# A two-layer graph attention and a transformer block on one core: a loop over batches written out from a table, wide products between the first batch's steps, setup work in other places

## The reference

```python
x = x + gat2(ctx_512, layernorm(x))      # adjacency = the normalised x
x = x + block(layernorm(x))

def gat_layer(x, adj, W, a_self, a_neigh, b):        # 8 heads of 32
    feat = einsum('nf,hfo->hno', x, W)
    e = (feat @ a_self)[:, :, None] + (feat @ a_neigh)[:, None, :]
    e = leaky_relu(e, 0.2) + -1e10 * (1.0 - adj)[None]
    out = softmax(e, -1) @ feat + b[:, None, :]
    return elu(out.transpose(1, 0, 2).reshape(256, 256))

# block: rmsnorm; q (16 heads of 128), k, v (4 heads); rmsnorm and rotary of q and k;
# causal attention; output projection; rmsnorm; gate of 8 experts, top 2;
# eight silu-gated experts of 176, mixed by the gate; residuals
```

## Time and profile before

| | |
|---|---|
| median of 3 runs | 676.4 us (676.07 to 676.8) |
| the profiled execution: time, span | 676.07 us, 676.1 us |
| instructions | 11574 |
| busy: TensorE, its weight loads | 604.8 us (89%), 445.9 us (66%) |
| busy: VectorE, ScalarE, GpSimd | 441.0 (65%), 266.7 (39%), 292.0 us (43%) |
| mean granted TensorE clock | 0.944 |
| moved by DMA | 14.51 MB, nearly all in the first 35 us |

### The profile page before, as it was taken

How to read it: one execution, slowest core, us unless ns; L and a number is a source line. 1 busy time by engine, 2 the same in 40 slices (tenths; PEclk the granted TensorE clock), 3 DMA queues, 4 the chain that set the end, 5 groups by cost and what they waited for, 6 DMA issues and landing times.

```text
span 676.1 us, 11574 instructions
## 1 busy us (share of the span) xinstructions
PE 604.8 (89%) x3140; PEld 445.9 (66%) x3140; DVE 441.0 (65%) x1277; ACT 266.7 (39%) x653; POOL 292.0 (43%) x588
## 2 busy tenths in 40 slices
PE   2786938979999998879999998879999998999998
PEld 1573933559678873558778973458777974676786
DVE  5727537975738756985738765986738766565363
ACT  2313305546533304636633304647633303674020
POOL 1514325885424023886425023886424126773000
PEclk9997558898999998979999998989999999999999
DMA  8900000000000000000000000000000000000000
GB/s 313 380 6 0 2 16 4 1 2 1 0 1 2 2 26 10 4 0 2 0 1 1 1 26 10 1 0 1 1 1 1 1 1 16 1 1 1 1 1 16
DMA packets 8305, 14.51 MB, mean 21 GB/s; under 512 B 860, under 2 KB 7068, under 8 KB 7988
## 3 DMA queue, kind: packets, MB, share of 16 engines
q1 hardware_dynamic: 8244, 13.76, 5.8%
HBM read 12.70 MB, written 1.05 MB: 20 GB/s over the span
## 4 chain that ended last, share of the span: by engine, by line
PE 56%; DVE 16%; issue 13%; POOL 9%; ACT 4%; POOLq 1%; DMA 1%; DVEq 0%; ACTq 0%; SPq 0%
PE bank L565 10%; PE bank L463 9%; PE ob L443 9%; PE bank L523 5%; PE tb L432 5%; PE bank L542 4%; DVE tt L904 3%; POOL m L775 2%; PE bank L538 2%; PE bank L534 2%; PE bank L509 2%; DVE lr L895 2%; PE zb L424 1%; ACT prob L666 1%; PE zb L414 1%
## 5 line engine op out<-in xcount | busy, mean ns | idle before, releaser
L735 POOL TENSOR_SCALAR tt<-tt,gmn 128x256 f32<-128x256 f32 x128 | 77.1, 613 | 64.1 <-DVE gmn L904 63.5
L509 PE MATMUL bank<-wqkv_sb,hT 128*128 128x512 f32 x192 | 97.9, 648 | 0.0
L666 ACT ACTIVATE prob<-bank,sneg,rms 128x128 f32<-128x128 f32 (+1 forms) x128 | 64.0, 507 | 68.5 <-DVE sneg L995 67.7
L775 POOL TENSOR_TENSOR m<-early,rope_s 128x256 f32<-128x256 f32 x80 | 70.8, 908 | 42.1 <-ACT early L647 41.8
L463 PE MATMUL bank<-m,wgu_sb 128*128 128x128 f32 (+1 forms) x480 | 86.6, 330 | 1.0 <-DVE m L1025 0.6
L791 POOL TENSOR_SCALAR prob<-prob,srcp 128x128 f32<-128x128 f32 (+1 forms) x128 | 53.7, 436 | 55.5 <-DVE srcp L1066 55.4
L463 PEld LDWEIGHTS bank<-m,wgu_sb 128*128 128x128 f32 x480 | 71.2, 191 | 9.2 <-issue 2.2
L443 PEld LDWEIGHTS ob<-feat,gpT 128*128 128x128 f32 x512 | 75.8, 227 | 0.8 <-issue 0.6
L443 PE MATMUL ob<-feat,gpT 128*128 128x33 f32 x512 | 75.2, 297 | 0.0
L895 DVE SCALAR_TENSOR_TENSOR lr<-zs 128x512 f32<-128x512 f32 x64 | 50.9, 797 | 25.3 <-ACT zs L625 22.6
L904 DVE CUSTOM_DVE_ANT_0 tt<-lr,maskv 128x256 f32<-128x256 f32 x128 | 62.3, 522 | 3.5 <-issue 2.9
(11 more groups left out here) (151 smaller groups left out, 1026.5 us busy)
## 6 DMA issues: line engine op xcount, KB each, us to landing
wqkv_sb<-wqkv_dram SPq DMA_DIRECT2D x1, 3072.0 KB, 12.4
wgu_sb<-wgu_dram SPq DMA_DIRECT2D x2, 1408.0 KB, 11.2
wo_sb<-wo_dram SPq DMA_DIRECT2D x1, 2048.0 KB, 17.8
wd_sb<-wd_dram SPq DMA_DIRECT2D x1, 1408.0 KB, 15.6
xin<-x_dram SPq DMA_DIRECT2D x4, 256.0 KB, 2.7
out_dram<-rows SPq DMA_DIRECT2D x8, 128.0 KB, 1.9
rows<-gat_rows_dram SPq DMA_DIRECT2D x1, 512.0 KB
cst<-consts_dram SPq DMA_DIRECT2D x1, 425.0 KB, 3.6
```

Source lines behind the costliest of these rows:

```text
L509: mm = pe.matmul(ps[:, :], hT[:, k, t * P:(t + 1) * P], wqkv_sb[:, k, c * G * HD:(c + 1) * G * HD], start=(k == 0), stop=(k == KT - 1))
L666: ins = act.activation(prob[:, n % 5, i * nk:(i + 1) * nk], ps[:, i * nk:(i + 1) * nk], ACT.Exp, bias=sneg[:, n, i:i + 1], scale=rq(g, t, ...
L735: ins = pool.tensor_scalar(tt[:, k % 3, h, :], tt[:, k % 3, h, :], -1.0, gmn[:, k % 3, h:h + 1], ALU.mult, ALU.add)
L775: ins = pool.tensor_tensor(dst[:, :, c, :], src[:, :, 1 - c, :], s_, ALU.mult)
```

## The change

- The loop is gone: a table `PLAN` lists ("gat", b, step), ("prep", b, step) and ("tail", b, step), and each engine issues its work by walking it. All semaphore values are constants. The order is the loop's, but what follows the second layer, now `prep`, is issued two steps earlier for batch 0 (`PREP_LEAD`).
- `keep_clock(n)` issues n products of 128x512 in bf16 into a bank that is not in use yet, after a step's `gat` work, for batch 0 alone: 127 in all, by the table `WAKE`.
- `apply_terms(1)` moves from after step 2 to after steps 14 and 15, one half of the weights each; the rotary tables and casts from after step 24 to after steps 25, 26 and 27. VectorE waits for the small loads at step 12.
- For batch 0 the three Newton rounds of the normalisation behind the layers are done on VectorE.
- `x1` and its statistics exist twice, the moments of that normalisation, `go`, `gT` have tiles of their own, `hn` lies in `m2`, `mixT` in `partsT`; the constants that only tables need are loaded into `x1[1]` and `hid` and not kept.

```diff
+SEQ, XS = (0, 1, 2, 3), 2
+PREP_LEAD = 2
+TERMS1_AT, ROPE_AT = (14, 15), (25, 26, 27)
+WAKE = {1: 2, 2: 4, 5: 2, 6: 2, 7: 2, 8: 14, 18: 5, 20: 3, 22: 3, 24: 6, 28: 3, 29: 3, 30: 3, 31: 12, 41: 18, 43: 6, 45: 3}
+WAKE.update({s: 2 for s in tuple(range(9, 18)) + tuple(range(32, 41))})
...
+PLAN = []
+for step in range(STEPS):
+    PLAN += [("gat", 0, step), ("prep", 0, step + PREP_LEAD)]
+for batch in range(B):
+    for step in range(STEPS):
+        PLAN += [("gat", batch + 1, step), ("prep", batch + 1, step)] if batch + 1 < B else []
+        PLAN += [("tail", batch, step)]
...
+            def keep_clock(n):
+
+                for _ in range(n):
+                    pe.matmul(bank[BANKS - 1][:, :], identb[:, :], identb[:, :].unsqueeze(1).broadcast_to([P, 4, P]), start=True, stop=True)
+
...
-            with pe.Fori(0, B - 1) as b:
-                for s in range(STEPS):
-                    gat(b + 1, s)
+            for what, b, s in PLAN:
+                if what == "gat":
+                    if b == 0 and s == TERMS_AT[1]:
+                        pe.wait_ge(setup_done, 2)
+                    gat(b, s)
+                    if b == 0:
+                        keep_clock(WAKE.get(s, 0))
+                elif what == "prep":
+                    prep(b, s)
+                else:
...
-                dve.wait_ge(dve_a, b * N_A + count[0])
+                dve.wait_ge(dve_a, count[0])
...
+                    if b == 0:
+                        for _ in range(3):
+                            newton(link_a, b, ln_y[:, :], ln_a[:, :], ln_v[:, :])
+                        dve.sem_inc(ln_ready, 1)
                     dve.sem_inc(ln_seed, 1)
...
+            def setup(s):
+
+                if s == UNIT_AT[0][-1]:
+                    dve.wait_ge(in_gat, 128)
+                if s in TERMS1_AT:
+                    apply_terms(1, TERMS1_AT.index(s))
+                if s == TERMS1_AT[1]:
+                    dve.sem_inc(setup_done, 1)
+                if s in ROPE_AT[:2]:
+                    rope_tables(ROPE_AT.index(s))
+                if s == ROPE_AT[2]:
+                    link(dve.tensor_copy(causal[:, :], causal_in))
+                    link(dve.tensor_copy(expert_rows[:, :], spread_in))
+                    dve.sem_inc(setup_done, 1)
...
-            for s in range(STEPS):
-                gat(0, s)
-                if s == PARTS_AT[0]:
-                    dve.wait_ge(in_gat, 80)
-                    apply_terms(1)
-                    dve.sem_inc(setup_done, 1)
-                if s == PARTS_AT[1]:
-                    rope_tables()
```

More of the change, by code:

```diff
@@ L43 @@
 C_TRI = C_NEIGH + 1
-C_END = C_TRI + E * E
+C_KEPT = C_TRI + E * E
+C_COS = C_KEPT
+C_SIN = C_COS + T * HD
+C_CAUSAL = C_SIN + T * HD
+C_END = C_CAUSAL + P
 def constants():
@@ L255, in block_program @@
         mixp = sb("mixp", [P, T, NP, E], BF16)
-        mixT = sb("mixT", [NP * E, N], BF16)
+        mixT = partsT[0:NP * E, :]
         th = pT1[:, :, :, :].rearrange("p m h q -> p (m h q)")[:, 0:3 * N].rearrange("p (a n) -> p a n", a=3)
@@ L361, in _ @@
             sp.dma_start(wd_sb[:, :, :], wd.rearrange("(j p) n -> p j n", p=P)).then_inc(in_d, 16)
[L363 to L374, removed]
             load_inputs(1)
-            with sp.Fori(0, B - 2) as b:
-                load_inputs(b + 2)
+            for b in range(B):
+                if b + 2 < B:
+                    load_inputs(b + 2)
                 store(b)
-            store(B - 2)
-            store(B - 1)
             sp.wait_ge(out_free, 16 * T * (B + 1))
@@ L600, in _ @@
                     long_products(b, s)
-            for s in range(STEPS):
-                for w in work(s):
-                    fill(B - 1, w)
-                long_products(B - 1, s)
         @block.scalar
@@ L682, in empty @@
                     act.activation(th[:, n % 3, :], ps[:, 0:N], ACT.Tanh, scale=0.5).then_inc(tanh_ready, 1)
-            for s in range(STEPS):
-                gat(0, s)
-            act.wait_ge(setup_done, 3)
-            with act.Fori(0, B - 1) as b:
-                for s in range(STEPS):
-                    gat(b + 1, s)
+            for what, b, s in PLAN:
+                if what == "gat":
+                    gat(b, s)
+                elif what == "tail":
+                    if b == 0 and s == 0:
+                        act.wait_ge(setup_done, 3)
                     for w in use(s):
                         empty(b, w)
-            for s in range(STEPS):
-                for w in use(s):
-                    empty(B - 1, w)
         @block.gpsimd
@@ L794, in _ @@
             pool.wait_ge(setup_done, 1)
-            for s in range(STEPS):
-                gat(0, s)
-            pool.wait_ge(setup_done, 3)
-            with pool.Fori(0, B - 1) as b:
-                links[0] = 0
-                for s in range(STEPS):
-                    gat(b + 1, s)
+            for what, b, s in PLAN:
+                if what == "gat":
+                    gat(b, s)
+                elif what == "prep":
+                    prep(b, s)
+                else:
+                    if b == 0 and s == 0:
+                        pool.wait_ge(setup_done, 3)
                     for w in use(s):
@@ L804, in _ @@
                     normalise(b, s)
-            assert links[0] == N_P, links
-            links[0] = 0
-            for s in range(STEPS):
-                for w in use(s):
-                    part(B - 1, w)
-                normalise(B - 1, s)
-        A_LINKS, B_LINKS = [0], [0]
         @block.vector
@@ new lines, in rope_tables @@
+            def rope_tables(m):
+                for t in range(T):
+                    w_ = qkw[:, m * HD:(m + 1) * HD]
+                    link(dve.tensor_tensor(rope_c[:, m, t, :], angles[:, t * HD:(t + 1) * HD], w_, ALU.mult))
+                    for c in range(2):
+                        half = slice(c * HD // 2, (c + 1) * HD // 2)
+                        sines = angles[:, (T + t) * HD + c * HD // 2:(T + t) * HD + (c + 1) * HD // 2]
+                        other = qkw[:, m * HD + (1 - c) * HD // 2:m * HD + (2 - c) * HD // 2]
+                        link(dve.tensor_tensor(rope_s[:, m, t, half], sines, other, ALU.mult))
@@ L1189, in _ @@
                     reciprocals(b, s)
-            assert count[1] == N_B, count
-            count[:] = [0, 0]
-            for s in range(STEPS):
-                for w in use(s):
-                    part(B - 1, w)
-                second_norm(B - 1, s)
-                reciprocals(B - 1, s)
+            assert count[1] == B * N_B, count
 def kernel(**inputs):
```

318 lines of the change are left out of this document (166 added, 152 removed).

## The result

The changed kernel takes 649.4 us (median of 4 runs, 647.07 to 652.13) against 676.6 us for the kernel before: a ratio of 0.958, 95% interval 0.954 to 0.962. The forecast was 644 us with a range of 634 to 661, so the direction and the range hold and the gain is 27 us where 32 were forecast. The profiled execution has 652.13 us and a span of 650.3 us. In the one of before, time and span are the same (676.07 and 676.1 us), so the two are set against each other stage by stage by spans: 676.1 less 650.3 is 25.8 us.

What follows compares the result with a forecast made beforehand. TensorE at half clock was taken to bound the first stretch, with a second loss at the loop's turns. Gains of 20.0 + 2.0 + 8.4 + 2.0 = 32.4 us from 676.1 gave 643.7, forecast as 644 us, range 634 to 661.

Steps and rivals of the forecast that it cites:

- layer 2: Second layer of batch 0: 21.0 us at full clock against 27.5, 6.5 us gained.
- the later pass's 0.44 and 0.81: Full-clock times in us of four transposes and eight 33-column products, against 1.04 and 1.55 at half clock.
- Layer 1: First layer of batch 0, earlier first leaky ReLU included: ends at 37.5 us against 45.9, 8.4 us gained.
- the 14: Wide products after step 8 in layer 1, expected at full clock, 0.24 us each; at half clock 3.4 us less gained.
- The start of pass 1: From the first stretch's end to the second key block's arrival on ScalarE: 2.0 us gained, bounds 0 and 2.7.
- The step "5.9": Start of pass 1 summed at full clock from terms, projections and part transposes: about 5.9 us, against 8.6 before.
- Turns: Starts of passes 2 and 3: without VectorE's wait 4.2 us less each, twice 8.4 us, bounds 5.0 and 9.
- tables: Second layer's weight terms moved to steps 14 and 15: first leaky ReLU 3.6 us earlier, at about 15.5 us.
- normalisation: First normalisation behind batch 0's layers, on VectorE: 2.0 us gained plus 0.6 on transposes at full clock, 2.6 us.
- Register steps: Register steps leaving all engines' queues with the loop: 0 to 6 us gained, 2.0 taken.
- change of layers: Between batch 0's two layers: the second layer's leaky ReLU moves up by 2.5 us, then waits for VectorE's tables.
- likeliest case: The prediction's own forecast of 644 us, chance 0.71, with bounds of its own, 635 to 654 us.
- the clock rises but doesn't hold: Rival: half of the first stretch stays at half clock, 3 us lost there, 669 us; chance 0.11.

Runs made afterwards that it cites:

- the run with early products: Changed kernel plus 11 wide products up to pass 1, 14 at the very start, 3 after steps 8 and 31: 656.6 to 658.2 us, one run 647.1.
- the densely filled version: Changed kernel plus 11 wide products up to pass 1, 16 at the start, more in TensorE's gaps, fewer after steps 8 and 31: 643.7 us, 0.945.
- the written-out run alone: Changed kernel with only the loop written out: no wide products, tables unmoved, Newton rounds on GpSimd, no two-step lead: 669.6 us, 0.987 of the kernel before.
- without the twos: Changed kernel without the two wide products after each of steps 9 to 17 and 32 to 40: 655.4 us, 0.963 of the kernel before.
- one for two: The run with early products, with one wide product instead of two after steps 9 to 17 and 32 to 40: 663.7 to 663.9 us, one run 649.3.

## Why the prediction was right, and where it was off

**The bound and the cure were right.** The first stretch was TensorE at half clock, with the earlier trace rows reading 1.00 over a layer that ran at half. The run without wide products brings half clock and 27.3 us back; with them layer 2 gains 7.0 us (6.5 forecast), priced from the later pass's 0.44 and 0.81.

**Layer 1 was mis-sized, by the case that the prediction named.** Forecast 8.4 us, 3.4 less if the 14 run at half clock; measured 5.3. The failed sentence is "TensorE is dense with wide products from about 12 us on, as before 57 us, so I expect full clock by the 14". It was dense from 12 us on, and the clock still rose only at 23.9, inside the 14. So keeping TensorE busy with wide products among narrow ones was not enough to raise it here: the run with early products kept it busy for 32.86 of 33.0 us at 0.50, two wide products a step among them. Which mix is enough, these runs don't settle. When the rise comes also differs between traces whose code is the same up to there: 23.9 us here, 23.4 and 21.5 in two others, with layer 1 at 25.0, 24.8 and 23.8 us. With the clock really up, in the densely filled version, layer 1 and the earlier ReLU gain 10.9 us (45.86 to 34.97). Ten products fewer ahead of the first transposes (4 for 14, 0.22 each) make 2.2 of this; the 8.7 left are close to the 8.4, so the sum was sound and only its clock was not.

**The start of pass 1 had the wrong sign, and the mechanism behind it had been seen.** Forecast +2.0 with bounds 0 and 2.7, measured -2.0. The step "5.9" at full clock was exact (5.87 and 5.88 where the clock held). The lower bound failed: "clock lost again while the last transposes are copied" was put at nothing, as before starts this pass at half clock too. But there the clock came back at 104.9 us, 5.7 after hT, and here at 92.1, 10.0 after. A clock lost just before this start cost more than one that was already about to return. Of the signs that the prediction named, the first leaky ReLU, the missing wait at the turns and passes 2 and 3 (148.7 and 148.9 us) came; 1.00 held only from 23.9 us, the first hT came at 82.1 instead of 79, and pass 1 took 152.3 us.

**Turns, tables and normalisation were right.** The turns gave 9.1 us (8.4 forecast), the tables 3.6, the normalisation 2.3 (2.6). That VectorE's wait plus the clock behind it is the price of a turn was worked out as 4.2 us. Making VectorE late in straight code reproduced the loop's 11.3 us starts in the profiled execution; the other three runs suggest about half of that price. The 5.9 us of a start without the wait hold as well: from the first term product to the copy, as the prediction counted, pass 2 took 5.8 (235.40 to 241.16). With the loop gone no block of instructions is loaded between 226 and 246 us, where the earlier trace rows has one; that VectorE waited for such a block is argued from this, no run varies it alone. The Trainium skill's 108 ns for a compare-and-branch ("Advanced Engine Details and Errata", Control Flow Timing) doesn't cover a turn here: taking the loop away gave 4.5 us at each.

**Register steps** were put at 2.0 us. All else together shrank by 1.6, but the written-out run alone shows 0.4 in pass 1, and in the other passes the places where the clock falls hide anything of this size. What the 1.6 is stays open.

**The sum.** 32.4 forecast, 25.8 by spans. Too much: layer 1 by 3.1, the start of pass 1 by 4.0, change of layers, normalisation and register steps by 0.8 together; too little: layer 2 by 0.5, the turns by 0.7. One sum of the prediction doesn't come out: the bounds of its likeliest case add up to 13.8 us above 643.7, which is 657.5 and not 654. The range of 634 to 661 is not touched by this.

**Of the rivals,** "the clock rises but doesn't hold" came true over 10 us, not over half the stretch; without the twos, or with gaps, it does come true.

## What to carry to other kernels

Where TensorE runs a long chain of narrow work at half clock, products on operands at hand can lift it, but they are free only in TensorE's idle gaps: a burst ahead of waiting work pays at half clock for the rise (5.57 us for the 14). Put them into the gaps from the rise to the stretch that carries itself, the last handoff included: with the clock lost again at 14.9 us, layer 1 took 32.84 us, more than the 27.25 without any products. And read a stretch's clock from the length of a known instruction before trusting a printed 1.00.

## What was not expected of the hardware

- A rise doesn't follow from a busy TensorE: 0.50 for 33 us at 32.86 us busy, with two wide products a step.
- The same program takes one of two times from run to run: with early products 647.1 us or 656.6 to 658.2, with one for two 649.3 or 663.7 to 663.9. The faster run has the higher mean granted clock (0.968 against 0.951 to 0.953, 0.960 against 0.933 to 0.936), so a clock kept or lost is the likely cause; the fast ones have no trace.
- What a low clock costs depends on where it lies. The start of pass 1 took 5.88 us at 1.00, 8.58 where the clock came back 5.7 us after hT (the kernel before), and 10.57 where it fell at 81.9 us, behind some 2.4 us of standing still, and came back 10.0 us after hT.
